# Layer 0's 3x3 convolution: nine taps shared out anew between TensorE, ScalarE and VectorE, with the last multiply on GpSimd

## What is computed

```python
xz = jnp.einsum('bhwc,ec->bhwe', x, in_proj_w)
xin, z = jnp.split(xz, 2, axis=-1)
xc = jnp.transpose(xin, (0, 3, 1, 2))
xc = lax.conv_general_dilated(xc, conv_w, (1, 1), [(1, 1), (1, 1)], feature_group_count=d, ...)
xc = jax.nn.silu(xc + conv_b[None, :, None, None])
...   # a selective scan in four directions over xc, a norm, a gate, a projection back
```

## Time and profile before

| | us |
|---|---|
| median of three runs | 8025.63 |
| lowest, highest | 8022.28, 8032.41 |
| the profiled run | 8029.31 |
| its span in the profile | 8027.5 |
| busy in the span: PE, DVE, ACT, POOL | 7204.7, 5968.8, 4079.6, 3653.2 |
| first image, PE's taps to the end of the last multiply | 38.74 to 80.57 |

### The profile page before, as it was taken

One profiled execution on the slowest core, in us unless ns is written; L12 is line 12 of the kernel. 1 busy time (PEld: TensorE's weight loads), 2 busy tenths in 40 slices (PEclk: granted clock), 3 DMA queues, 4 the chain that ended last, 5 costly groups with the idle time before them and its releaser, 6 DMA issues. The chain is left out here.

```text
span 8027.5 us, 170490 instructions
## 1 busy us (share of the span) xinstructions
PE 7204.7 (90%) x62522; PEld 6194.8 (77%) x62522; DVE 5968.8 (74%) x9085; ACT 4079.6 (51%) x8541; POOL 3653.2 (46%) x4036
## 2 busy tenths in 40 slices
PE   7999889998999989999756788879897999999999
PEld 6888768886788867888546666735666999999899
DVE  7999879998899978999734555545556767767677
ACT  5887668875688856887411222224443222222222
POOL 4888558885588846888455555411000000000000
PEclk9999999999999999999878889989998999999999
DMA  2333223332233322333365555400003434434343
GB/s 61 91 92 92 70 65 91 92 91 70 65 91 94 90 64 73 90 93 91 99 173 167 165 158 151 130 6 3 1 0 94 130 115 124 124 116 124 116 125 111
DMA packets 590220, 762.24 MB, mean 95 GB/s; under 512 B 51687, under 2 KB 527880, under 8 KB 587569
## 3 DMA queue, kind: packets, MB, share of 16 engines
q1 hardware_dynamic: 537777, 584.54, 24.7%
q0 software_dynamic: 51840, 169.91, 7.4%
HBM read 720.59 MB, written 33.66 MB: 94 GB/s over the span
## 5 line engine op out<-in xcount | busy, mean ns | idle before, releaser
L630 POOL TENSOR_TENSOR l_arena<-l_arena 128x768 f32<-128x768 f32 x1536 | 2591.6, 1688 | 452.4 <-DVE l_arena L562 446.6
L562 DVE TENSOR_TENSOR_SCAN l_arena<-l_arena,psum 128x772 f32<-128x772 f32 x1536 | 2662.7, 1750 | 176.8 <-PE psum L394 72.6
L487 ACT ACTIVATE l_arena<-l_arena,l_A 128x384 f32<-128x384 f32 x3072 | 1642.5, 603 | 36.1 <-DVE l_arena L562 32.8
L396 PE MATMUL psum<-l_arena 128*128 128x128 f32 x11520 | 1497.5, 280 | 47.7 <-DVE l_arena L562 44.1
L396 PEld LDWEIGHTS psum<-l_arena 128*128 128x128 f32 x11520 | 1365.8, 192 | 171.3 <-issue 147.9
L407 PE MATMUL psum<-l_ident,l_arena 128*128 128x128 f32 x9216 | 1257.6, 273 | 50.6 <-ACT l_yT L493 41.7
L407 PEld LDWEIGHTS psum<-l_ident,l_arena 128*128 128x128 f32 x9216 | 1055.1, 141 | 60.2 <-POOL l_arena L630 60.2
L2247 POOL TENSOR_TENSOR st_mab<-st_xr 128x384 f32<-128x384 f32 x8 | 7.8, 998 | 2045.4 <-DVE st_xr L2237 2045.4
L1189 POOL DMA_INDIRECT l_G<-neighbours,l_idx x648 | 619.5, 956 | 668.0 <-PE psum L1237 334.0
L477 ACT ACTIVATE l_arena<-l_arena,l_BT 128x256 f32<-128x256 f32 x1728 | 746.7, 496 | 7.5
L2522 ACT ACTIVATE st_own_s<-psum 128x384 f32<-128x384 f32 x256 | 125.7, 491 | 1091.2 <-PE psum L2359 1091.2
(11 more groups left out here) (435 smaller groups left out, 11297.0 us busy)
## 6 DMA issues: line engine op xcount, KB each, us to landing
l_arena<-c_rows SPq DMA_DIRECT2D x1536, 192.0 KB, 3.0
st_FS<-filter_sums SPq DMA_DIRECT2D x128, 1155.0 KB, 9.5
st_F<-filter_parts SPq DMA_DIRECT2D x128, 320.5 KB, 7.0
neighbours<-l_xt SPq DMA_DIRECT2D x256, 72.0 KB
st_mab<-in_st_mp SPq DMA_DIRECT2D x68, 256.0 KB, 9.3
st_mab<-in_st_mm SPq DMA_DIRECT2D x68, 256.0 KB, 6.2
l_G<-neighbours,l_idx POOLq DMA_INDIRECT x648
l_gnx<-in_x SPq DMA_DIRECT2D x4, 1152.0 KB, 5.7
```

Source lines behind the costliest of these rows:

```text
L396: mm = pe.matmul(ps[:, o:o + P], dtuT[:, g % 2, t, h * P:(h + 1) * P], diagB[:, rank[s] % 3, t, :], start=True, stop=True)
L487: act.activation(decay[:, s % NDC, half(h)], dtv[:, g % 2, h, :], ACT.Exp, scale=A[:, g // NRC, h, n:n + 1]).then_inc(s_exp, 1)
L562: dve.tensor_tensor_scan(hbuf[:, n, run], decay[:, s % NDC, run], x2_ps[s % 2][:, run], 0.0, ALU.mult, ALU.add).then_inc(s_scan, 1)
L630: pool.tensor_tensor(hC[:, s % NHC], halves(hbuf[:, s % NS, :]), Cs[:, s % NCS, :].unsqueeze(1).broadcast_to([P, 2, RC]), ALU.mult).then_i ...
```

## The change

`NTE` becomes 4. PE makes taps 0 to 3. ACT makes tap 4 with the bias (`first_tap`, an Identity activation with a scale and a bias for each partition, which writes `xc`), two chunks ahead, from its own queue behind the twelve copies; `s_t0` counts it. DVE makes taps 5 to 8, all four as SCALAR_TENSOR_TENSOR with a wait behind each, then the sum. POOL does the multiply by the sigmoid, and `s_silu` counts it for ACT, which reuses a place of `sig` when the multiply two chunks back is done.

```diff
--- before.py
+++ after.py
@@ -64,7 +64,7 @@
 RC = 384
 NRC = L // RC
 PW = WW + 2
-NTE = 5
+NTE = 4
 LB = RC // P
 NCH = KD * NRC
 NSTEP = NCH * NS
@@ -163,7 +163,8 @@
                 dve.tensor_scalar(A[:], A[:], -1.0, None, ALU.mult)
 
         s_x, s_a, s_v, s_gm, s_px = (sem(n) for n in ("x_loaded", "act_step", "dve_step", "gn_mean", "xin_made"))
-        s_cv, s_cs, s_tap, s_mz = (sem(n) for n in ("conv_made", "conv_summed", "tap_added", "pad_zeroed"))
+        s_cv, s_cs, s_tap, s_mz, s_t0, s_silu = (sem(n) for n in (
+            "conv_made", "conv_summed", "tap_added", "pad_zeroed", "first_tap_made", "silu_made"))
         scan_sem = Semaphores(nc, ctx, "l0s_")
         s_id, s_rows, s_lo, s_dtp, s_btp, s_bt, s_sf, s_dt, s_du, s_tp, s_tc = (scan_sem(n) for n in (
             "ident_laid", "rows_made", "rows_copied", "dt_projected", "B_turned", "B_copied", "softplus_step", "dt_made",
@@ -183,13 +184,16 @@
             with nc.Block() as block:
                 NPB = 2 * NRC
 
+                def rows(ap):
+                    return ap.rearrange("p (y x) -> p y x", y=8)
+
                 @block.sync
                 def _(sp):
                     sp.dma_start(gnx[:], x_in[:, ds(b * L, L)]).then_inc(s_x, 16)
 
                 @block.vector
                 def _(dve):
-                    st = Steps(dve, s_v, b * (NRC + 6 + NPB))
+                    st = Steps(dve, s_v, b * (NRC + 6))
                     dve.wait_ge(s_x, 16 * b + 16)
                     for i in range(NRC):
                         st.mark(dve.bn_stats(stats[:, i, :], gnx[:, i * RC:(i + 1) * RC]))
@@ -206,39 +210,17 @@
                     dve.wait_ge(s_a, b * (2 + 2 * NPB) + 2)
                     st.mark(dve.tensor_scalar(gnx[:], gnx[:], gst[:, 0:1], gst[:, 3:4], ALU.subtract, ALU.mult))
 
-                    def rows(ap):
-                        return ap.rearrange("p (y x) -> p y x", y=8)
-
-                    def silu(n):
-                        h, c = n // NRC, n % NRC
-                        xs = xc[:, h, c * RC:(c + 1) * RC]
-
-                        dve.wait_ge(s_a, b * (2 + 2 * NPB) + 2 + NPB + n + 1)
-                        st.mark(dve.tensor_tensor(xs, xs, sig[:, n % 2, :], ALU.mult))
-
                     for n in range(NPB):
                         h, c = n // NRC, n % NRC
                         xs = xc[:, h, c * RC:(c + 1) * RC]
-                        if c == 0:
-
-                            dve.wait_ge(s_a, b * (2 + 2 * NPB) + 2 + (h + 1) * NRC)
-
-                        for t in range(NTE, 9):
+                        dve.wait_ge(s_t0, b * NPB + n + 1)
+                        for t in range(NTE + 1, 9):
                             src = xpad[:, h, 8 * c + t // 3:8 * c + t // 3 + 8, t % 3:t % 3 + WW]
-                            if t == NTE:
-                                ins = dve.tensor_scalar(rows(xs), src, conv_w[:, h, t:t + 1], conv_b[:, h:h + 1], ALU.mult, ALU.add)
-                            else:
-                                ins = dve.scalar_tensor_tensor(rows(xs), src, conv_w[:, h, t:t + 1], rows(xs), ALU.mult, ALU.add)
-                            ins.then_inc(s_tap, 1)
-                            if t + 1 < 9:
-                                dve.wait_ge(s_tap, (b * NPB + n) * (9 - NTE) + t - NTE + 1)
-                        if n:
-                            silu(n - 1)
-                        dve.wait_ge(s_tap, (b * NPB + n + 1) * (9 - NTE))
+                            dve.scalar_tensor_tensor(rows(xs), src, conv_w[:, h, t:t + 1], rows(xs), ALU.mult, ALU.add).then_inc(s_tap, 1)
+                            dve.wait_ge(s_tap, (b * NPB + n) * (8 - NTE) + t - NTE)
                         dve.wait_ge(s_cv, b * NPB + n + 1)
                         dve.tensor_tensor(xs, xs, ps[:, BANK * (4 + n % 4):BANK * (4 + n % 4) + RC], ALU.add).then_inc(s_cs, 1)
-                    silu(NPB - 1)
-                    assert st.n == NRC + 6 + NPB
+                    assert st.n == NRC + 6
 
                 @block.scalar
                 def _(act):
@@ -254,23 +236,38 @@
                         at.mark(act.activation(xpad[:, h, 1 + 8 * c:9 + 8 * c, 1:1 + WW],
                                                ps[:, BANK * (1 + n % 3):BANK * (1 + n % 3) + RC].rearrange("p (y x) -> p y x", y=8),
                                                ACT.Copy))
+                    def first_tap(n):
+                        h, c = n // NRC, n % NRC
+                        if c == 0:
+                            act.wait_ge(s_a, b * (2 + 2 * NPB) + 2 + NPB)
+                        act.activation(rows(xc[:, h, c * RC:(c + 1) * RC]),
+                                       xpad[:, h, 8 * c + NTE // 3:8 * c + NTE // 3 + 8, NTE % 3:NTE % 3 + WW],
+                                       ACT.Identity, bias=conv_b[:, h:h + 1], scale=conv_w[:, h, NTE:NTE + 1]).then_inc(s_t0, 1)
+
+                    first_tap(0)
+                    first_tap(1)
                     for n in range(NPB):
                         h, c = n // NRC, n % NRC
+                        if n + 2 < NPB:
+                            first_tap(n + 2)
                         act.wait_ge(s_cs, b * NPB + n + 1)
                         if n >= 2:
-
-                            act.wait_ge(s_v, b * (NRC + 6 + NPB) + NRC + 6 + n - 1)
+                            act.wait_ge(s_silu, b * NPB + n - 1)
                         at.mark(act.activation(sig[:, n % 2, :], xc[:, h, c * RC:(c + 1) * RC], ACT.Sigmoid))
 
                 @block.gpsimd
                 def _(pool):
                     pool.memset(xpad[:], 0.0).then_inc(s_mz, 1)
+                    for n in range(NPB):
+                        xs = xc[:, n // NRC, n % NRC * RC:(n % NRC + 1) * RC]
+                        pool.wait_ge(s_a, b * (2 + 2 * NPB) + 2 + NPB + n + 1)
+                        pool.tensor_tensor(xs, xs, sig[:, n % 2, :], ALU.mult).then_inc(s_silu, 1)
 
                 @block.tensor
                 def _(pe):
                     pe.wait_ge(s_gm, 2 * b + 1)
                     pe.matmul(ps[:, 0:2], gmat[:], m2[:], start=True, stop=True).then_inc(s_p1, 1)
-                    pe.wait_ge(s_v, b * (NRC + 6 + NPB) + NRC + 6)
+                    pe.wait_ge(s_v, (b + 1) * (NRC + 6))
                     for n in range(NPB):
                         h, c = n // NRC, n % NRC
                         if n >= 3:
```

## The result

| | before | after |
|---|---|---|
| median, seven runs each, us | 8025.63 | 8055.21 |
| lowest, highest | 8018.53, 8041.94 | 8044.71, 8068.57 |
| ratio of the two | | 1.0033, 95% interval 1.0021 to 1.0044 |
| span of the profiled execution | 8027.5 | 8053.4 |
| stage, PE's first tap to the next block, each image | 42.08 to 42.12 | 46.46 to 46.48 |

The account below looks back on a forecast made before the run. DVE's chain was taken to bound layer 0's stage. Stage terms and set-up gave -8.5 us, 44 multiplies at 0.9 us gave +39.6: 8025.6 + 31.1 = 8056.7 us; own range 8052 to 8066, with rivals 8016 to 8066.

Parts of the forecast that it names:

- What bounds the stage: Layer 0's tap stage: DVE has no idle time, 3.285 us a chunk before; it stays the bound after the change.
- PE's gain: PE's taps in the stage: 0.65 us a chunk gained, off the path, buying nothing.
- a chunk without the conflict: DVE's four chained taps and sum: 3.09 us against 3.285, saving 2.15 us an image over 11 chunks.
- First sum: Start of the stage: first sum 0.37 us earlier in each image; DVE's lost early start costs nothing.
- table load: Before the first ACT tap: priced at nothing; 1.28 us an image, 5 us in all, kept as upper end.
- The price of a multiply: POOL's multiply beside DVE's taps, both reading two SBUF tensors: holds DVE 0.9 us each, +39.6 us in all.
- Tail: End of the stage: last multiply on POOL takes 0.99 us against 0.56 and starts later, +0.49 us an image.
- Set-up: Products of the identity with tap weights, eight instead of ten: saves 0.4 us once, on the path.
- rival (c): PE's clock falls to 1.2 GHz within the stage, eight records take 5.2 us a chunk: up to +84 us, chance 0.03.
- rival (d): Faster by over 0.2%: needs 0.36 us a chunk more than DVE's chain of waits allows; chance 0.02.
- Rival (a): DVE takes its SBUF turn first and isn't held up by POOL's multiply: 8017, or 8022 with table load; chance 0.20.
- (b): POOL and DVE share the port finely, both stretched, DVE losing some 0.4 us a chunk: 8035; chance 0.14.

Follow-up runs that it names:

- The two kernels with PE kept busy: The change with 19 more matmuls ending PE's taps, 7776.3 us, and the kernel before with 4 more, 7748.2 us, both against 7758.1 us.
- the kernel with one column: The change with POOL multiplying only the first column of each chunk by the sigmoid; 8024.0 us, ratio 1.0003 to the kernel before.
- The doubled multiply: The change with POOL making each multiply twice, the first into a scratch place; stage 54.2 us, sums 4.31 us apart.
- the three kernels with PE kept busy: Extra matmuls ending PE's taps: 19 on the change (ratio 1.0025), 4 on the kernel before (0.9990), 6 on a version alternating two chunks on DVE (0.9974).
- the pairs without extra matmuls: The change with DVE alternating two chunks' taps, multiplying again and starting after six copies; 7739.0 us against the kernel before's 7758.1.

## Why the prediction was right, and where its steps were off

The time, 8055.2 against 8056.7 us, is closer than the working deserves, and that is luck: the stage was put 14 us too high, and 8 to 12 us outside the stage were put at nothing.

- **What bounds the stage.** Right. DVE's chain sets the chunk, and PE's gain is off the path: a chunk without the conflict takes 3.08 us where 3.09 had been worked out.
- **First sum.** Right in kind: -0.27 us, not -0.37. ACT's tap takes 0.694 us and not the 0.604 of the earlier trace rows; it has a bias for each partition besides the scale. No table load stood before it: the copy starts at 38.04 and the tap at 38.56. The early start that DVE lost had indeed been idle time.
- **The price of a multiply.** The mechanism is what the working said, down to which tap is long: POOL waits for the second tap, the third waits for POOL, 1.24 us. The size was off: 0.62 us and not 0.9, so the long tap is 1.24 us and not 1.5, and sums are 3.70 us apart and not 4.0. The lowest price that I allowed, 0.84 us, takes 0.15 us off POOL's recorded time for the part ahead of its reading, which the runs bear out (0.14), but nothing for a part behind it; together it is 0.37 us. For 44 multiplies that is 12 us too much.
- **Tail.** +0.10 us and not +0.49. From the last sigmoid's start to the end of the multiply it is +0.48, as reckoned, but that sigmoid now follows the last sum by 0.59 us and not 0.97, which I had not looked into. It is not POOL's doing: with the multiply back on DVE it is 0.58 too. The kernels in which ACT waits for the multiply by `s_silu` have 0.58 to 0.59, those in which it waits by `s_v` 0.94 to 0.97; why isn't known.
- **Set-up.** The products take 1.66 us instead of 2.05, as reckoned, but they begin 0.30 us later, behind a DMA, and the first statistics, which wait for the image's DMA, start at 19.64 instead of 19.66. In the traces of the other runs they start between 19.02 and 19.86, so 0.4 us cannot be seen there.
- **So the stage** was forecast at +7.9 us an image and measures +4.4: 17.5 us in all, where 31.5 had been reckoned.
- **Outside the stage.** This is the step that failed. Of PE's faster taps I wrote that they buy nothing; they cost. PE is through 13.9 us before the block's end, its clock falls while it is idle, and the scan's block begins at 1.2 GHz in all four images. I had weighed the clock only within the stage (rival (c), which did not come: PE kept its full clock until its last tap). The two kernels with PE kept busy show both signs of it. What the runs show of its size is 4 us: the way to the first scan, 79.7 against 75.6 us over four images. The two profiles lie 25.9 us apart, of which 17.5 are the stages and 4.0 this way. Another 1.5 us lie between the statistics and PE's first tap, where the first one to three steps between ACT's copies are 1.28 us and the others 0.65; how many are long differs from image to image, in the kernel before too. And 2.4 us come from the second image alone, which in the kernel before takes 907.3 us from the first scan to the next statistics, 909.6 and 909.7 in its neighbours and 909.5 to 909.8 in the change. No run ties these to the change. They may be scatter, and so may the rest of the 8 to 23 us of the kernel with one column, whose way to the first scan is 3.4 us longer than before; this stays open.
- **Two sums.** The forecast's own range should begin at 8054: 44 x 0.84 - 8.5 = +28.5 us, and 8052 was written. In rival (d) 0.36 us a chunk is the whole of 16 us; beyond the 8.5 us already counted, 0.17 would have been missing. Neither changes the range.
- **Rival (a)**, that DVE goes first each time, and **(b)**, that both are stretched, fall with the first profile: one tap of 1.24 us in each chunk, the others at 0.61 to 0.62. The doubled multiply confirms it: one more long tap, of the same length.

## What to carry to other kernels

Moving an elementwise step from VectorE to GpSimd did not free VectorE here, where both read two SBUF tensors: the step cost VectorE 0.62 us as a guest and, filling a gap of its chain, 0.34 us as its own work (3.42 against 3.08 us a chunk). Give GpSimd work that only writes, or put it beside VectorE instructions that read PSUM. And when an engine with a clock that depends on its work is made to finish early, look at what comes after the barrier: relieving TensorE inside a stage made the start of the next one 2 us longer in two images of four, and matmuls whose result nobody reads gave that back.

## What the runs showed of the hardware

- A POOL multiply holds up a DVE tap with two SBUF inputs for its own recorded time less 0.37 us, 0.62 us for 128x384 and 0.21 us for 128x192; filling with zeros holds nothing.
- A SCALAR_TENSOR_TENSOR behind one that it must wait for costs 0.655 us, and 0.53 us when another stands between them.
- An activation of 128x384 from SBUF takes 0.694 us with a scale and a bias for each partition (Identity), 0.604 with the scale alone (Exp at L487), 0.524 with neither (the sigmoid).
- PE's clock at the beginning of the scan's block, by the time that PE had been idle ahead of it: full in all twelve images after 0.3, 0.6 or 1.6 us (the three kernels with PE kept busy); after 3.1 us (the kernel before) full in two images and at the lower level in two; at the lower level in all images after 4.0, 6.3, 7.7, 11.8 and 13.9 us (the pairs without extra matmuls, only the multiply moved, one column, the multiply on DVE, the change).
